# The down projection of a transformer layer: pairs of token tiles by seven block products instead of eight

## What is computed

```
h = s4d_kernel(...)                       # 16 x 128 x 1024: 2048 tokens of 1024 features
h = h + attention(layernorm(h))
x = layernorm(h)
g = x @ w_gate.T + 0.02 * (x @ gate_A @ gate_B)     # w = (q - 7.5) * scale * 0.005, q in 0..15
u = x @ w_up.T   + 0.02 * (x @ up_A @ up_B)
hid = silu(g) * u                         # 2048 x 2752
out = h + hid @ w_down.T + 0.02 * (hid @ down_A @ down_B)
```

## Time and profile before

| | us |
|---|---|
| median of 3 runs (1929.54 to 1933.36) | 1930.83 |
| the profiled execution | 1929.66 |
| its span in the profile | 1927.9 |
| PE, DVE, POOL, ACT busy | 1805.6, 1197.5, 859.1, 712.6 |
| down stage: first to last matmul | 1618.1 to 1923.8 |

### The profile page before, as it was taken

How to read it: one execution, slowest core, us unless ns; L and a number is a source line. 1 busy time by engine, 2 the same in 40 slices (tenths; PEclk the granted TensorE clock), 3 DMA queues, 4 the chain that set the end, 5 groups by cost and what they waited for, 6 DMA issues and landing times.

```text
span 1927.9 us, 31412 instructions
## 1 busy us (share of the span) xinstructions
PE 1805.6 (94%) x12892; PEld 984.2 (51%) x12892; DVE 1197.5 (62%) x1570; ACT 712.6 (37%) x1026; POOL 859.1 (45%) x593
## 2 busy tenths in 40 slices
PE   0586999999999999999999999999999999999999
PEld 0575665656666655545554344444444444444444
DVE  8996577787878888855656876675755554111111
ACT  4477243343433344432114645454544443000000
POOL 6973134343333434432361577664777774011111
PEclk9998999999999999999999999999999999999999
DMA  2122111111122221144532343434465454434341
GB/s 97 43 67 68 62 56 22 34 37 43 47 58 64 80 75 63 67 147 163 168 121 67 98 132 99 131 113 139 142 195 172 156 164 147 154 106 150 113 143 44
DMA packets 102704, 194.92 MB, mean 101 GB/s; under 512 B 14305, under 2 KB 75489, under 8 KB 92065
## 3 DMA queue, kind: packets, MB, share of 16 engines
q1 hardware_dynamic: 102560, 192.90, 31.2%
HBM read 135.72 MB, written 56.11 MB: 100 GB/s over the span
## 4 chain that ended last, share of the span: by engine, by line
PE 75%; DVE 9%; POOL 2%; issue 2%; ACT 2%; DMA 0%; DVEq 0%; ACTq 0%
PE acc L1514 15%; PE acc L1380 12%; PE acc L1382 12%; PE ps_p L1172 4%; PE ps_p L1174 4%; PE ps_p L1173 4%; PE acc L1286 3%; PE acc L1287 3%; PE ps_t L1199 3%; PE acc L1288 3%; PE ps_p L1188 2%; PE ps_p L1190 2%; PE ps_p L1189 2%; PE ps_l L1389 2%; POOL prob L1061 1%
## 5 line engine op out<-in xcount | busy, mean ns | idle before, releaser
L1061 POOL TENSOR_TENSOR prob<-prob,mx 128x1024 f32<-128x1024 f32 x64 | 121.4, 1897 | 371.5 <-DVE mx L1883 371.5
L1172 PE MATMUL ps_p<-x_hi,w_qk 128*128 128x512 f16 x512 | 194.7, 380 | 0.0
L1173 PE MATMUL ps_p<-x_lo,w_qk 128*128 128x512 f16 x512 | 194.0, 379 | 0.0
L1174 PE MATMUL ps_p<-x_hi,w_qk 128*128 128x512 f16 x512 | 194.0, 379 | 0.0
L2270 DVE TENSOR_TENSOR y<-acc,down_scale 128x1024 f32<-128x1024 f32 (+1 forms) x17 | 19.7, 1162 | 253.0 <-PE acc L1514 253.0
L1114 POOL TENSOR_TENSOR hidden<-up,hidden 128x512 f16<-128x512 f32 x80 | 91.1, 1160 | 144.8 <-ACT hidden L1740 144.6
L1162 POOL TENSOR_TENSOR lr_term<-lr_term,h_again 128x1024 f32<-128x1024 f32 x16 | 37.6, 2347 | 253.6 <-ACT lr_term L1830 253.6
L1188 PE MATMUL ps_p<-w_v,x_hi 128*128 128x256 f16 x512 | 140.5, 274 | 4.8 <-PEq L806 3.6
L1066 POOL TENSOR_TENSOR prob<-prob,sm 128x1024 f32<-128x1024 f32 x64 | 120.2, 1897 | 52.9 <-DVE sm L1890 52.9
L1189 PE MATMUL ps_p<-w_v,x_hi 128*128 128x256 f16 x512 | 140.4, 274 | 0.0
L1190 PE MATMUL ps_p<-w_v,x_lo 128*128 128x256 f16 x512 | 140.4, 274 | 0.0
(11 more groups left out here) (343 smaller groups left out, 4367.7 us busy)
## 6 DMA issues: line engine op xcount, KB each, us to landing
q_raw<-in_gu_q SPq DMA_DIRECT2D x42, 1024.0 KB, 6.2
hid_parts<-hidden_parts SPq DMA_DIRECT2D x16, 1376.0 KB, 6.7
hidden_parts<-hidden SPq DMA_DIRECT2D x42, 512.0 KB, 3.5
down_raw<-in_down_q SPq DMA_DIRECT2D x22, 512.0 KB, 3.6
w_raw<-in_w_qk SPq DMA_DIRECT2D x8, 1024.0 KB, 5.0
h_tokens<-n_tok SPq DMA_DIRECT2D x16, 512.0 KB, 3.7
o_parts<-ot SPq DMA_DIRECT2D x32, 256.0 KB, 2.3
wv_raw<-in_w_o SPq DMA_DIRECT2D x8, 1024.0 KB, 4.8
```

The lines of the kernel that those rows point to most:

```text
L1061: nc.gpsimd.tensor_tensor(prob[s % 2][p][:], prob[s % 2][p][:], bc(mx[p][:], H, 2), ALU.subtract).then_inc(s_sub[p], 1)
L1172: nc.tensor.matmul(out[:], w[:, j % 2, m, 0, at], xn_hi[:, k, tok], start=(k == 0), stop=False)
L1173: nc.tensor.matmul(out[:], w[:, j % 2, m, 0, at], xn_lo[:, k, tok], start=False, stop=False)
L1174: last = nc.tensor.matmul(out[:], w[:, j % 2, m, 1, at], xn_hi[:, k, tok], start=False, stop=(k == KT - 1))
```

## The change

Tiles 0 and 1 are computed as before (with `low_term(1)` behind block 10). Tiles 2 to 15 are taken in pairs q = 1 to 7, tile n = 2q and m = 2q + 1. The inner blocks 0 to 9 and 10 to 19 and the two column halves make a 2 x 2 block product, which needs seven products of 20 matmuls instead of eight. Blocks 20 and 21 are plain (`down_rest`, 3 matmuls for each tile and half). The operands are sums: four of `hid` tiles (made in float32, and split in two float16 parts in `dsum`), four of levels (exact in float16).

The listing below is condensed: the calls and waits are those of the diff, in its order, with set-up and repeated conditions told in words or left out.

Order on PE in a pair: p1, low_term(n), p22, p2, p6, p5, p7, p3, low_term(m), p4. DVE reads the banks in the order c11, x22, v, x5, x7, c12 and, at the beginning of the next pair, c21. Hid sums of 128x640 elements, in halves h = 0, 1: POOL makes sum 1 (`hid_one`, 3 operations) and sum 3 (`hid_three`, 3), DVE sums 2 and 4 (2 operations each), ACT the high part, DVE the low part. Level sums of 128x512: 1 and 4 and six of 2 on DVE, 3 and four of 2 on POOL. Those of `hid` for pair q + 1 are made during pair q, those for pair 1 and the level sums during tiles 0 and 1 and pair 1.

More of the change, by code:

```diff
@@ L540 @@
 TWICE = (6, 12, 18)
+KD = 10
+DP = C // 2
+DOWN_PROD = ("p1", "p22", "p2", "p6", "p5", "p7", "p3", "p4")
+DOWN_READ = ("c11", "x22", "v", "x5", "x7", "c12", "c21")
+BY_POOL = 4
 NJ = len(JOBS)
@@ L1513, in down @@
                     for b in halves:
-                        last = nc.tensor.matmul(acc[n % 2][:, b, :], parts[n % 3][:, at], levels[i][:, b * CH:(b + 1) * CH],
+                        last = nc.tensor.matmul(acc[n % 2][:, b, :], parts[n][:, at], levels[i][:, b * CH:(b + 1) * CH],
                                                 start=(i == 0 and part == 0), stop=(i == FULL))
@@ L1534, in _, with down_block @@
         down(0, 16, IT).then_inc(s_main, 1)
-        for n in range(1, C - 1):
-            down(n, 0, IT // 2)
-            low_term(n)
[L1538 to L1542, removed]
+        down(1, 0, KD).then_inc(s_half, 1)
+        low_term(1)
+        down(1, KD, IT).then_inc(s_main, 1)
+        def down_block(bank, of_hid, of_levels, adds, ends):
+            for i in range(KD):
+                for part in two:
+                    last = nc.tensor.matmul(banks[bank], of_hid(i, part), of_levels(i), start=(not adds and i == 0 and part == 0),
+                                            stop=(ends and i == KD - 1 and part == 1), skip_group_check=adds)
+            return last
@@ L2262, in _, with scale_sums @@
         hidden(NJ - 1, 0)
[L2264 to L2271, removed]
+        def scale_sums(n):
+            dve.wait_ge(s_main, n + 1)
+            tt(y[n][:], acc[n][:].rearrange("p b n -> p (b n)"), scl_d[:], ALU.mult).then_inc(s_y1, 1)
@@ new lines, in add_first, with low_hid_sum, sum_two_hid @@
+        def add_first(n):
+            dve.wait_ge(s_y1, n + 1)
+            dve.wait_ge(s_sum, n + 1)
+            tt(y[n][:], y[n][:], lrt[n][:], ALU.add).then_inc(s_y, 1)
+        def low_hid_sum(q, k, h, src):
+            dve.wait_ge(s_dh[k], 2 * (q - 1) + h + 1)
+            tt(piece(dsum[k][1], h), src[:], piece(dsum[k][0], h), ALU.subtract).then_inc(s_dl[k], 1)
+        def sum_two_hid(q, h):
+            to = f2[h]
+            dve.wait_ge(s_f1, 2 * (q - 1) + h + 1)
+            dve.wait_ge(s_parts[2 * q % 4], 16 * (2 * q // 4 + 1))
+            if q > 1:
+                dve.wait_ge(s_dl[3], 2 * (q - 2) + h + 1)
+            chain.after(tt(to[:], f1[h][:], hid_piece(2 * q, 0, h, 0), ALU.subtract))
+            tt(to[:], to[:], hid_piece(2 * q, 0, h, 1), ALU.subtract).then_inc(s_f2, 1)
@@ L2272, in scale_sums, with scaled, add_term @@
+        left, right = slice(0, CH), slice(CH, D)
+        def scaled(to, cols):
+            chain.mark(tt(to[:, cols], to[:, cols], scl_d[:, cols], ALU.mult))
+        def add_term(n, cols):
+            chain.wait()
             dve.wait_ge(s_sum, n + 1)
             tt(y[n % 2][:, cols], y[n % 2][:, cols], lrt[n % 2][:, cols], ALU.add).then_inc(s_y, 1)
+        def last_down(q):
+            sum_down(q, "c21", "p4", 1, y[1][:, left], first_d[:], None)
+            dve.wait_ge(s_dread, dread(q, "c21"))
+            scaled(y[1], left)
@@ L2283, in _ @@
-        scale_sums(C - 1, 1, True)
+        scale_sums(0)
+        for h in two:
+            sum_two_hid(1, h)
+        dve.wait_ge(s_half, 1)
+        for i in range(KD - BY_POOL):
+            dve.wait_ge(s_l3, i + 1)
+            tt(level_sum(2, i), level_sum(3, i), level_block(0, 0, i), ALU.add).then_inc(s_l2, 1)
+        scale_sums(1)
+        for k in (1, 0):
+            for h in two:
+                low_hid_sum(1, k, h, (f1, f2)[k][h])
+        add_first(0)
+        add_first(1)
+        for i in range(KD):
+            if i < KD - BY_POOL:
+                dve.wait_ge(s_l2, i + 1)
+            else:
+                dve.wait_ge(s_l2_pool, i + 1 - (KD - BY_POOL))
+            tt(level_sum(4, i), level_block(1, 0, i), level_sum(2, i), ALU.subtract).then_inc(s_l4, 1)
@@ new lines, in _ @@
+        for q in range(1, DP):
+            if q > 1:
+                last_down(q - 1)
+                add_term(2 * q - 1, slice(0, D))
+            for h in two:
+                three_and_four(q, h)
+            for h in two:
+                low_hid_sum(q, 3, h, f2[h])
+            dve.wait_ge(s_yout[0], 16 * q)
+            dve.wait_ge(s_dprod, dprod(q, "p2"))
+            tt(y[0][:, left], banks[0], scl_d[:, left], ALU.mult).then_inc(s_dread, 1)
+            dve.wait_ge(s_dfirst, q)
+            dve.wait_ge(s_yout[1], 16 * q)
+            sum_down(q, "x22", "p22", 3, y[1][:, right], first_d[:], None)
+            if q + 1 < DP:
+                sum_two_hid(q + 1, 0)
+            sum_down(q, "v", "p6", 1, y[0][:, right], first_d[:], None)
+            if q + 1 < DP:
+                sum_two_hid(q + 1, 1)
+                low_hid_sum(q + 1, 1, 0, f2[0])
+            sum_down(q, "x5", "p5", 2, y[1][:, right], y[1][:, right], "x22")
+            if q + 1 < DP:
+                for h in two:
+                    low_hid_sum(q + 1, 0, h, f1[h])
+                low_hid_sum(q + 1, 1, 1, f2[1])
+            sum_down(q, "x7", "p7", 1, y[1][:, right], y[1][:, right], "x5")
+            dve.wait_ge(s_dread, dread(q, "x7"))
+            scaled(y[1], right)
+            sum_down(q, "c12", "p3", 2, y[0][:, right], y[0][:, right], "v")
+            dve.wait_ge(s_dread, dread(q, "c12"))
+            scaled(y[0], right)
+            add_term(2 * q, slice(0, D))
@@ L2284, in layer @@
+        add_term(C - 1, right)
+        last_down(DP - 1)
+        add_term(C - 1, left)
     block_stack.close()
```

189 lines of the change are left out of this document (158 added, 31 removed).

## The result

The changed kernel takes **1939.98 us** (median; before, 1930.83): 1.0045 of the time before, interval [1.0033, 1.0056]. The profiled execution has a span of 1939.1 (before 1927.9) at a granted clock of 0.986. Medians count every execution, while the ratios leave out four slow ones, one each of the changed kernel (3286.06 us), e2 (6315.36), e4 (7008.61) and e6 (2554.08; the only profile of e6, which is therefore not read).

A forecast was written before the change was run, and what follows sets the result against it. TensorE alone was taken to bound the down stage. -30.2 + 4.5 + 21.5 + 5 x 3.3 + 1.9 + 0.7 = +14.9 on 1930.8 gave 1945.7, stated as 1945.5 us; range 1918 to 1957, eight in ten.

The forecast's parts named there:

- Removed, -30.2: Seven pairs need 152 matmuls for 172; 140 go at 0.216 us each, -30.2 us.
- The turns: DVE operations with both inputs in SBUF alternate with POOL's on a shared path; 34.8 us asked per 33.8 us pair.
- p2 behind the copy, +4.5: Pair 1: p2 waits for first_down(1), which stands on ACT behind the copy of hid_three(1); 4.5 us.
- v, +21.5: Pair 1: p7 waits for v, behind everything else in DVE's queue, in turns with POOL; 21.5 us.
- Slow clock, +1.9: Behind the stall in pair 1, some eighteen matmuls at a lowered TensorE clock run 0.105 too long each; 1.9 us.
- Middle pairs, +3.3 each: Pairs 2 to 6: p3 waits 1.9 for x5 and p4 1.4 for x7; a pair takes 37.1 us.
- The end, +0.7: After the last matmul stand three operations (c21, scaled, addition) where there were two; +0.7 us.
- The base: Starting time for the sum: profiled execution 1929.66, median of the runs 1.17 above it, 1930.8 us.
- no turns: Rival: DVE and POOL work side by side, in pair 1's preparation and every middle pair; -26.1, 1904.7 us; chance 0.10.
- whole instructions held: Rival: holds last the whole recorded instruction, a turn 1.85 for 1.56; 25.9 us on top, 1971.6; chance 0.06.
- middle pairs absorb it: Rival: p5 to p3 wait for nothing, only the first pair pays; -1.6, 1929.2 us; chance 0.12.
- level sums 4 run free: Rival: POOL starts the next pair's hid_one late, so six turns of 1.31 leave DVE's queue; -9.5, 1921.3; chance 0.08.

The follow-up runs named there:

- e2: Changed kernel with the ten level sums 4 moved behind x5 of pair 1: 1935.31 us.
- e4: Changed kernel with the first half of the second hid sum (`hid_f20`) in PSUM: 1928.61 us.
- e6: Changed kernel with the edits of e4 and e2 together: 1921.75 us.
- e1: Changed kernel with all VectorE sums except level sums reading one input from PSUM (output values wrong): 1912.77 us.
- e12: Changed kernel with only the order in a pair changed, x5 and x7 ahead of low halves for the next pair: 1936.80 us.
- e9: e7 with four plain tiles, so seven products only from pair 2 on: 1917.23 us.
- e3: Changed kernel with GpSimd's sums for pair 2 held until v of pair 1 is read, VectorE's pair 1 order changed too: 1940.16 us.
- e7: e6 with x5 and x7 put ahead of sums that only the next pair wants: 1916.55 us.
- e8: Changed kernel with tiles 2 and 3 also computed plainly, seven products from pair 2 on: 1934.56 us.
- e10: e11 with GpSimd's sums for pair 2 also held until VectorE has the fourth sums of pair 1: 1920.22 us.
- e11: e7 with, in pair 1, the copy ahead of ACT's high halves and v ahead of the sum for pair 2: 1919.39 us.
- e13: Changed kernel with the odd tile's parts loaded in two halves, the first early, ahead of p3's wait: 1937.40 us.

## Why the prediction was right, point by point

The forecast was +14.9 over the kernel before; the medians say +9.2, the stage in the profiles +7.9. Sign and mechanism hold; every wait stands where it was put, and p6 and p5 wait for nothing. The sizes are less good. The forecast counted its waits from the time when a matmul was due; counted so, the copy, v and the middle pairs cost 3.2, 17.4 and 12.5 us for 4.5, 21.5 and 16.5, each too long in the forecast, and the slow clock, 2.0 more than forecast, took back a part. With the measured terms the sum is -30.2 + 3.2 + 17.4 + 12.5 + 3.9 + 0.7 = +7.5.

- *Removed, -30.2.* Right. Pair 7, with nothing to prepare, takes 33.95 for 33.8, and e1, with only 8.5 us of waits, has a stage 18.6 us shorter than before.
- *The turns.* Right, and shown by e1. A turn of both takes 1.94 for 1.99. Copies of 640 on ACT took 0.73 for 0.75.
- *p2 behind the copy, +4.5.* It was 3.0. "The clock after p2's wait costs nothing" was half wrong: between 1665.0 and 1684.6 the clock was 0.91 and the 63 matmuls there took 15.2 for 13.6. It did no harm because p7 waited for v anyway, as the sentence said. e12 had the same wait and no slow clock behind it.
- *v, +21.5.* The single wait most off: 17.3. v ended 41.1 after the pair's start for 44.9. Of the 3.8, 3.0 were there at the end of level sums 4 (23.7 for 26.7): the two additions ended 1.3 sooner and the ten sums took 8.2 for 9.9. The rest of the walk to v, eight sums of hid, y0 left, x22 and two sums more, was 17.4 for 18.2. p7 was due 0.3 later in its pair (23.8 for 23.5), which makes 4.1.
- *Slow clock, +1.9.* The granted clock was 0.64 in the gap and 0.50 from 1701.9 to 1706.0 (1.2 GHz); p7 and p3, 43 matmuls, took 11.6 for 9.3: +2.3. With the 1.6 behind p2 it is 3.9, of which the 1.6 came before v's wait and are inside its shortened length.
- *Middle pairs, +3.3 each.* 2.2 of waiting as listed, 1.1 and 1.1 in the mean for 1.9 and 1.4, and 2.5 with the 0.16 of each; a pair takes 36.3 for 37.1. In pair 3 POOL began 8.1 us after the pair's start for 6.7, but with DVE between sums it met fewer turns and ended hid_one(0) at 12.9 as forecast; x5 came at 24.7 for 25.2.
- *The end, +0.7.* 0.65. There DVE also waited 2.3 for POOL's last term, in time for the last matmul.
- *The base.* The stage began 3.3 us later than in the profile before. It moves between executions also of kernels with the same code, and the medians do not need it: 7.9 and 9.2 differ by little more than 1. Where it begins at 1621.4 or later (changed, e2, e4, e9) the granted clock from 100 to 200 us was 0.84 to 0.86, where it begins before 1619 (the kernel before, e1, e3, e7, e8, e12) 0.88 to 0.91. What sets that clock was not tested.

The rivals: *no turns* fell by 1.94 and e1; *whole instructions held* by the same 1.94 for 2.22; *middle pairs absorb it* by ten waits; *level sums 4 run free* by six of them at 1211 ns in the mean and not 410. Four of the ten ran free, as the forecast had it, and POOL was out of work from 1682.0.

## What to carry to other kernels

Before giving VectorE and GpSimd work to save TensorE's, add up what both ask of the path that they share, not the busy share of each; here 34.8 us for 33.8 said that each middle pair would be late. It did not say by how much: the excess is 1.0, the pairs waited 2.2 as listed, and 1.3 in the better order of e12. Where the sum is near full, holding one engine back only moves a wait (e3, e10), a later place of work gives back a part of it (e2) or nothing (e11), an earlier start or an earlier load gives little (e8, e13), and one input in PSUM takes the work off the path for good (e1, e4). Then put ahead in the queue what TensorE wants next (e7).

## Not expected of the hardware

- PSUM frees a VectorE operation of the turns only as an input: 1838 ns with the output there and both inputs in SBUF, 813 to 832 with an input there.
- The fp16 sums of 128x512 took 0.41 us alone, the fp32 ones 0.69; in turns level sums 4 and 2 took 1.21 and 1.61 in the mean, so the gain is lost beside GpSimd.
- What the slow clock costs behind a TensorE gap did not grow with the gap. Behind gaps from 2.1 us (e10) to 18.9 us (e12) the matmuls took 1.4 to 3.0 us too long: in the changed kernel 2.3 behind 17.3 and 1.6 behind 3.0, in e3 3.0 behind 3.3. Behind the 3.0 of e12 they took no longer at all.
